# A graph attention layer's softmax taken over two batches at once, with the engines' order rewritten in pairs of batches

## The reference

```python
h = relu(layernorm(x))
q, k, v = h @ Wq + bq, h @ Wk + bk, h @ Wv + bv          # 4 heads x 32
alpha = (q[dst] * k[src]).sum(-1) / sqrt(32)             # per edge and head
ea = exp(alpha - segment_max(alpha, dst)[dst])
alpha = ea / (segment_sum(ea, dst)[dst] + 1e-16)
x = x + segment_sum(v[src] * alpha, dst) + h @ Wskip + bskip
h = relu(layernorm(x))
x = x + layer1(h, src, dst, edge_attr)
```

## Time and profile before

| | us |
|---|---|
| median of 3 runs | 1698.16 (1695.48 to 1698.21) |
| the profiled execution | 1695.94 |
| its span, first to last instruction | 1694.1 |
| PE busy | 1487.4 (88%) |
| DVE busy | 1347.4 (80%) |
| ACT busy | 1005.7 (59%) |
| POOL busy | 981.1 (58%) |

### The profile page before, as it was taken

One profiled execution on the slowest core, in us unless ns is written; L12 is line 12 of the kernel. 1 busy time (PEld: TensorE's weight loads), 2 busy tenths in 40 slices (PEclk: granted clock), 3 DMA queues, 4 the chain that ended last, 5 costly groups with the idle time before them and its releaser, 6 DMA issues.

```text
span 1694.1 us, 37116 instructions
## 1 busy us (share of the span) xinstructions
PE 1487.4 (88%) x12117; PEld 1382.1 (82%) x12118; DVE 1347.4 (80%) x3855; ACT 1005.7 (59%) x2472; POOL 981.1 (58%) x1021
## 2 busy tenths in 40 slices
PE   5877898598999999999999973899999999999996
PEld 4655676487888888888888863899999999999896
DVE  8989898288999999999999993666666666666664
ACT  5665787565665555566555521656656666565663
POOL 0110000277777777777777703777777777777772
PEclk9998999799999999999999995999999999999998
DMA  8786898746666666666666624676676766767662
GB/s 219 246 260 219 269 311 253 221 137 178 183 186 175 191 178 179 181 181 179 169 187 173 178 68 108 144 173 156 157 171 156 174 158 157 171 154 172 154 165 58
DMA packets 162139, 302.88 MB, mean 179 GB/s; under 512 B 104024, under 2 KB 107514, under 8 KB 156985
## 3 DMA queue, kind: packets, MB, share of 16 engines
q1 hardware_dynamic: 121089, 201.19, 41.3%
q0 software_dynamic: 40896, 99.90, 24.2%
HBM read 196.84 MB, written 104.12 MB: 178 GB/s over the span
## 4 chain that ended last, share of the span: by engine, by line
PE 24%; DVE 24%; POOL 18%; issue 18%; ACT 10%; DMA 4%; SPq 1%; DVEq 0%; POOLq 0%; ACTq 0%
POOL sb_kv L753 15%; PE ps_b L1572 5%; ACT sb_hn L1497 4%; ACT sb_vw L1500 4%; DVE sb_st L1115 3%; DVE sb_xo L1101 3%; PE ps_b L1669 3%; PE ps_b L1648 3%; POOL sb_kv L726 3%; DVE sb_member L1029 2%; DVE sb_alpha L1049 2%; DVE sb_kv L828 2%; DMA sb_kv<-in_x 2%; DVE sb_st L809 2%; PE ps_b L1561 2%
## 5 line engine op out<-in xcount | busy, mean ns | idle before, releaser
L726 POOL DMA_INDIRECT sb_kv<-kv_rows,sb_src_all x500 | 495.5, 991 | 375.8 <-DMA kv_rows<-sb_kv 215.3
L753 POOL DMA_INDIRECT sb_kv<-x_rows,sb_src_all x500 | 472.9, 946 | 213.9 <-issue 142.1
L1497 ACT ACTIVATE sb_hn<-sb_xn 100x128 f32<-100x128 f32 x500 | 240.4, 481 | 265.2 <-DMA sb_kv<-x_rows,sb_src_all 172.1
L1210 DVE COPY sb_hT<-ps_b 128x400 f32<-128x400 f32 x250 | 142.8, 571 | 135.0 <-PE ps_b L1757 133.8
L1425 ACT ACTIVATE sb_hn<-sb_xn,sb_nstat 100x128 f32<-100x128 f32 x500 | 231.6, 495 | 15.5 <-DMA sb_xn<-in_x 15.5
L1500 ACT ACTIVATE sb_vw<-sb_kv 128x128 f32<-128x128 f32 x500 | 239.5, 479 | 0.0
L1572 PE MATMUL ps_b<-sb_w,sb_memberT 128*125 128x256 f32 x800 | 206.4, 397 | 31.2 <-DVE sb_kv L828 18.8
L1771 PE MATMUL ps_b<-sb_w,sb_hT 128*100 128x128 f32 x1000 | 198.4, 280 | 9.7 <-DVE sb_hT L1210 9.4
L1447 ACT COPY sb_memberT<-ps_b 100x512 f32<-100x512 f32 x150 | 76.0, 507 | 207.5 <-PE ps_b L1657 207.5
L1773 PE MATMUL ps_b<-sb_weaug,sb_memberT 66*100 66x128 f32 x1000 | 193.7, 275 | 0.0
L1772 PE MATMUL ps_b<-sb_w,sb_hT 128*100 128x128 f32 x1000 | 193.3, 275 | 0.0
(11 more groups left out here) (165 smaller groups left out, 3066.4 us busy)
## 6 DMA issues: line engine op xcount, KB each, us to landing
kv_rows<-sb_kv SPq DMA_DIRECT2D x27, 1120.0 KB
x_rows<-sb_xo SPq DMA_DIRECT2D x25, 1015.6 KB
sb_xn<-x_rows SPq DMA_DIRECT2D x50, 507.8 KB
sb_xn<-in_x SPq DMA_DIRECT2D x50, 500.0 KB
out_rows<-sb_xo SPq DMA_DIRECT2D x50, 500.0 KB
sb_kv<-in_edge_attr SPq DMA_DIRECT2D x500, 32.0 KB
sb_kv<-in_x SPq DMA_DIRECT2D x28, 560.0 KB
kv_rows<-sb_xn SPq DMA_DIRECT2D x13, 1120.0 KB
```

Source lines behind the costliest of these rows:

```text
L726: pool.indirect_dma_start(out=kvs[:, k % 4, t, :], out_offset=None, in_=kv_rows, in_offset=bass.IndirectOffsetOnAxis(ap=src_all[:, n:n + 1 ...
L753: pool.indirect_dma_start(out=xs1[:, k % 4, t, :], out_offset=None, in_=x1, in_offset=bass.IndirectOffsetOnAxis(ap=src_all[:, n:n + 1], ax ...
L1497: nc.scalar.activation(hn1[:, t, :], xn1[:, k % 4, t, 0:D], ACT.Relu, scale=xn1[:, k % 4, t, D:D + 1], bias=xn1[:, k % 4, t, D + 1:XW]).th ...
```

## The change

Batches are taken in pairs (`DUOS` = 25). `alpha`, the softmax tiles and the weights have 80 rows (`TWO`) instead of 40, for batches 2p and 2p + 1; turn_alpha, the eight softmax steps, the exp, turn_weights and the load of the segment rows happen once a pair. The weighed values are written over the keys of their slot in `kvs`, so `vw` goes, and its memory holds a fourth slot of `member`. The slot in `kvs` is free for the next gather when its batch has been summed, not when it has been weighed. The offset of q is no longer a matmul in project_q: q gets a 101st row that holds bq and the turned member matrix a 101st row of ones, and gather_q contracts over 101 rows. Two DMAs write these rows once. VectorE's and TensorE's order is written anew as `second_scores(p)` and `weighed_sums(p)`; ScalarE's keeps its order but for the exp.

In this diff the old `step0` of VectorE and of TensorE, and the likewise renamed arguments of `soft_step` are left out.

```diff
+TWO = 2 * BH
+DUOS = BATCHES // 2
...
+        bqb = sb("bqb", [1, D])
...
-        qsb = q_raw[0:NODES, :].rearrange("n (s t c) -> n s t c", s=2, t=B)
-        memberT = mT_raw[0:NODES, :].rearrange("n (s t e) -> n s t e", s=2, t=B)
+        qsb = q_raw[0:NODES + 1, :].rearrange("n (s t c) -> n s t c", s=2, t=B)
+        memberT = mT_raw[0:NODES + 1, :].rearrange("n (s t e) -> n s t e", s=2, t=B)
         member = mem_raw[:].rearrange("e (s t n) -> e s t n", s=4, t=B)
-        vw = vw_raw[:].rearrange("e (t c) -> e t c", t=B)
+        member_3 = vw_raw[:, 0:B * NODES].rearrange("e (t n) -> e t n", t=B)
...
-        alpha = sb("alpha", [128, BH])
-        segk = sb("segk", [BH, 2, SEG])
-        fmax = sb("fmax", [BH, WIN])
-        smax = sb("smax", [BH, WIN])
-        dl = sb("dl", [BH, WIN])
-        er = sb("er", [BH, WIN])
-        fsum = sb("fsum", [BH, WIN])
-        tot = sb("tot", [BH, WIN])
-        tot_e = sb("tot_e", [BH, WIN])
-        rtot = sb("rtot", [BH, WIN])
-        wr = sb("wr", [BH, WIN])
+        alpha = sb("alpha", [128, TWO])
+        segk = sb("segk", [TWO, 2, SEG])
...
+        def member0(k):
+
+            return member[:, k % 4, :, :] if k % 4 < 3 else member_3
...
+            sp.dma_start(bqb[:], bq.rearrange("(o n) -> o n", o=1)).then_inc(const_load, 16)
...
-            def segments(k):
-                wait(sp, A.soft, N_SOFT * (k - 1))
-                if k == 0:
+            def segments(p):
+                wait(sp, A.soft, N_SOFT * (p - 1))
+                if p == 0:
                     sp.wait_ge(seg_out, 16)
-                rows = seg_rows[B * k:B * (k + 1), :].unsqueeze(1).to_broadcast([B, HEADS, SEG])
-                sp.dma_start(segk[:, k % 2, :], rows).then_inc(A.seg[k % 2], 16)
+                rows = seg_rows[2 * B * p:2 * B * (p + 1), :].unsqueeze(1).to_broadcast([2 * B, HEADS, SEG])
+                sp.dma_start(segk[:, p % 2, :], rows).then_inc(A.seg[p % 2], 16)
...
+            for k in range(5):
                 nodes(k)
-            for k in range(2):
-                segments(k)
-            for k in range(BATCHES + 2):
-                if k == BATCHES:
+            segments(0)
+
+            sp.wait_ge(P.hT, 3 * PB)
+            sp.dma_start(q_raw[NODES:NODES + 1, :].rearrange("o (n c) -> o n c", c=D),
+                         bqb[:].unsqueeze(1).to_broadcast([1, 2 * B, D])).then_inc(rows_set, 16)
+            sp.wait_ge(P.kv, 5 * PB)
+            sp.dma_start(mT_raw[NODES:NODES + 1, :].rearrange("o (n c) -> o n c", c=D),
+                         ones[0:1, :].unsqueeze(1).to_broadcast([1, 2 * B, D])).then_inc(rows_set, 16)
+
+            for p in range(DUOS + 1):
+                if p == DUOS - 1:
                     first_windows = window_registers(0)
-                if k >= 1 and real(k + 1):
-                    segments(k + 1)
-                if k >= 3 and k % 2 == 1:
-                    store((k - 3) // 2)
-                if real(k + 4):
-                    nodes(k + 4)
+                if p + 1 < DUOS:
+                    segments(p + 1)
+                if p >= 1:
+                    store(p - 1)
+                for k in (2 * p + 5, 2 * p + 6):
+                    if real(k):
+                        nodes(k)
...
-                wait(pool, A.vw, k - 3)
+                wait(pool, A.agg, 3 * (k - 3))
...
-                wait(dve, A.agg, 3 * (k - 2))
-                dve.tensor_tensor(member[:, k % 3, first:last, :],
+                wait(dve, A.agg, 3 * (k - 3))
+                dve.tensor_tensor(member0(k)[:, first:last, :],
...
+                wait(dve, A.aT, k // 2)
+                dve.tensor_reduce(alpha[:, BH * (k % 2):BH * (k % 2 + 1)], prod.rearrange("e t (h c) -> e (t h) c", h=HEADS), AX_X, ALU.add
...
             def weigh(k):
-                dve.wait_ge(A.wT, k + 1)
-                wait(dve, A.agg, 3 * k)
-                dve.tensor_tensor(vw.rearrange("e t (h c) -> e (t h) c", h=HEADS),
+                dve.wait_ge(A.wT, k // 2 + 1)
+                dve.wait_ge(A.prod, 3 * (k + 1))
+                weights = banks[5][:, BH * (k % 2):BH * (k % 2 + 1)]
+                dve.tensor_tensor(kvs[:, k % 4, :, 0:D].rearrange("e t (h c) -> e t h c", h=HEADS),
                                   kvs[:, k % 4, :, D:2 * D].rearrange("e t (h c) -> e t h c", h=HEADS),
-                                  banks[5][:, 0:BH].rearrange("e (t h) -> e t h", h=HEADS).unsqueeze(3)
+                                  weights.rearrange("e (t h) -> e t h", h=HEADS).unsqueeze(3)
                                   .to_broadcast([128, B, HEADS, CH]), ALU.mult).then_inc(A.vw, 1)
...
+            def second_scores(p):
+                k = 2 * p + 1
+                def stats(first, last):
+                    if p >= 1:
+                        for n in range(first, last):
+                            x1_stat_step(p - 1, n)
+                def build(part):
+                    if real(k + 2):
+                        members(k + 2, part)
+                scores(k, 0)
+                stats(0, 1)
+                scores(k, 1)
+                stats(1, 2)
+                scores(k, 2)
+                stats(2, 3)
+                head_sums(k)
+                stats(3, 4)
+                build(0)
+                stats(4, 5)
+                soft_step(p, 0)
+                stats(5, 6)
+                soft_step(p, 1)
+                stats(6, 7)
+                soft_step(p, 2)
+                stats(7, 8)
+                build(1)
+                stats(8, 9)
+                soft_step(p, 3)
+                stats(9, 10)
+                soft_step(p, 4)
+                stats(10, 11)
+                soft_step(p, 5)
+                stats(11, 12)
+                soft_step(p, 6)
+                stats(12, 13)
+                soft_step(p, 7)
+                stats(13, 14)
+            def weighed_sums(p):
+                k = 2 * p
+                nxt = real(k + 2)
+                weigh(k)
+                weigh(k + 1)
+                finish(k, 0)
+                finish(k, 1)
+                x1_stats(k, 0)
+                x1_stats(k, 1)
+                finish(k, 2)
+                x1_stats(k, 2)
                 if nxt:
+                    scores(k + 2, 0)
+                    scores(k + 2, 1)
+                finish(k + 1, 0)
                 if nxt:
+                    scores(k + 2, 2)
+                    head_sums(k + 2)
+                finish(k + 1, 1)
+                x1_stats(k + 1, 0)
+                x1_stats(k + 1, 1)
+                finish(k + 1, 2)
+                x1_stats(k + 1, 2)
+                if real(k + 4):
+                    members(k + 4, 0)
+                    members(k + 4, 1)
+            for k in range(3):
+                members(k, 0)
+                members(k, 1)
+            for g in range(3):
+                scores(0, g)
+            head_sums(0)
+            for p in range(DUOS):
+                second_scores(p)
+                weighed_sums(p)
+            for n in range(STAT_STEPS):
+                x1_stat_step(DUOS - 1, n)
...
+            def exps(p):
+                act.wait_ge(A.soft, N_SOFT * p + 3)
...
-                if real(k - 1):
-                    exps(k - 1)
...
+                if real(k) and k % 2 == 1:
+                    exps(k // 2)
...
-                nc.tensor.matmul(ps[0:NODES, 0:(last - first) * D].rearrange("n (t c) -> n t c", c=D),
-                                 ones_b[:, 0:NODES], bsplit[:, 0:D].unsqueeze(1).to_broadcast([128, last - first, D]),
-                                 start=True, stop=False)
                 for t in range(first, last):
                     ins = nc.tensor.matmul(ps[0:NODES, (t - first) * D:(t - first + 1) * D], hnT[:, k % 3, t, :],
-                                           w0[:, 0, :], start=False, stop=t == last - 1)
+                                           w0[:, 0, :], start=True, stop=True)
...
+                if a == 0:
+                    pe.wait_ge(rows_set, 32)
...
+            def turn_alpha(p):
+                pe.wait_ge(A.alpha, 2 * (p + 1))
+                wait(pe, A.vw, 2 * p)
+                nc.tensor.transpose(banks[5][0:TWO, 0:WIN], alpha[:], ident[:]).then_inc(A.aT, 1)
+
+            def turn_weights(p):
+                pe.wait_ge(A.soft, N_SOFT * (p + 1))
+                nc.tensor.transpose(banks[5][:, 0:TWO], wr[:], ident[0:TWO, 0:TWO]).then_inc(A.wT, 1)
...
-                    ins = nc.tensor.matmul(ps[0:NODES, (t - first) * D:(t - first + 1) * D], member[:, k % 3, t, :],
-                                           vw[:, t, :], start=False, stop=t == last - 1)
+                    ins = nc.tensor.matmul(ps[0:NODES, (t - first) * D:(t - first + 1) * D], member0(k)[:, t, :],
+                                           kvs[:, k % 4, t, 0:D], start=False, stop=t == last - 1)
...
+            def second_scores(p):
+                k = 2 * p + 1
+                nxt = real(k + 1)
+                gather_q(k, 2)
```

(48 more changed lines are left out.)

134 lines of the change are left out of this document (28 added, 106 removed).

## The result

| | before | changed |
|---|---|---|
| device time, median (lowest to highest) | 1696.82 us (1692.55 to 1698.21, 4 runs) | 1717.23 us (1716.07 to 1722.52, 4 runs) |
| ratio to before, with its 95% interval | 1 | 1.0122 [1.0106, 1.0137] |
| profiled execution: time, span | 1695.94, 1694.1 us | 1716.89, 1715.1 us |
| VectorE, TensorE, GpSimd busy, 600 to 700 us | 97.49, 93.92, 75.47 us | 83.62, 88.14, 72.54 us |
| one pair of batches, weighing to weighing | 26.94 us, one of 24 30.46 (mean over the layer 27.05) | 27.65 us, four of 23 29.0 to 29.2 (mean 27.91) |

The changed kernel is 1.2% slower.

A forecast was written before the change was run, and what follows sets the result against it. VectorE paces now; changed, a loop through TensorE: 23.1 work + 4.8 stalls + 0.05, 28.0 us a pair. 360.3 + 672.0 - 4.2 + 17.3 = 1045.4, 15.2 later: 1711.1 us profiled, 1713 against the median; range 1692 to 1738.

The forecast's parts named there:

- the third rival: The 80-row softmax costs twice the 40-row one, so VectorE saves nothing: loop about 29.5 us, time 1749; chance 0.03.
- (e): TensorE's turn_member(2p + 2, 2) waits for ScalarE's copy of the first four turned members: 0.64 us + 0.10.
- (d): TensorE's turn_alpha waits for the odd batch's scores and head sums: 0.31 us + 0.10.
- (a): TensorE's first aggregate waits for VectorE's weighing, no longer covered by two skips: 1.61 us, 1.71 with the weight load.
- (b): TensorE's q gather of batch 2p + 3's second four tiles waits for ScalarE's copy: 1.18 us + 0.10.
- (c): TensorE's project_q(2p + 2, 0) waits for the copy of h, without an offset matmul ahead: 0.39 us + 0.10.
- (f): TensorE's skip(2p, 2) waits for a sum: 0.14 us.
- TensorE's work, put at 23.1 us: TensorE's work for two batches: 24.6 us now, less 1.5 for the q offset and the dropped turns.
- The second rival: The clock falls in the loop behind stall (a), costing 1.7 us each; 1734 in half the pairs, 1755 in all; chance 0.18.
- an edge between 1.65 and 1.85 us: In layer 1 the clock fell after a 1.85 us stall, not after 1.65; (a) would show as about 1.6.
- the next half sentence: If the two row copies on SP's queue were late, the first q gather would wait, once.
- The tail: From the last weighing to layer 0's last layer norm step: 17.3 us, 2 of them for a falling clock.

The follow-up runs named there:

- The two runs that removed a stall each: Changed kernel with TensorE's two skips moved behind the turned weights: 1704.65 us; changed kernel with ScalarE's member copies ahead of three ReLUs: 1703.55 us.
- the run that removed both: Changed kernel with row copies ahead of later node loads, skips behind the turned weights and ScalarE's copies ahead of the ReLUs: 1672.55 us, the fastest.
- the run that put one into the kernel before: Kernel before with TensorE's two skips ahead of the turned weights instead of behind them: 1783.09 us, ratio 1.0502.

## Why the prediction was right, and where it was off

**The bound.** That VectorE's share would fall and the time rise was right, and for the reason given: the engines form a closed loop through TensorE. The two runs that removed a stall each, the run that removed both and the run that put one into the kernel before show this from four sides.

**What is taken away.** The 80-row steps have the length of the 40-row ones (the reciprocal 0.95 us, a scan 0.41), the weighing in place takes 1.49, both as taken, so the third rival is out. The offset's 1.2 us for two batches (1.1 in the run that puts it back) showed as 0.60 in the pair's length; part of the rest fell on waits, of which (e) shows 0.1 us less in that run.

**The stalls.** The view shows a wait about 0.15 us short, and one that would show as less than 0.15 not at all; so (d) has no wait of TensorE in the list above. Its weight load shows it, in each of the 20 pairs:

```profile
PEld ps_b L1708 <- DVE sb_alpha L1066: 7.2, 20, 0.5
```

From start to start, less the time of the instruction ahead, the stalls are: (a) 1.63 us where 1.61 was counted, (b) 1.06 for 1.18, (c) 0.40 for 0.39, (d) 0.31 for 0.31, (e) 0.65 for 0.64, (f) 0.17 for 0.14. In sum that is 4.22 for 4.27, so the path was right, and of the sizes only (b) is off by more than 0.03. The weight load behind a stall is open: the twelve matmuls behind (b) take 1.44 us to the next group (664.43 to 665.87), sixteen without a stall 1.79, which makes 1.34 for twelve: 0.10, as estimated. The Trainium skill (TensorE: Matmul & The Clock Gate, Part 2) has the next load pulled ahead of running matmuls; behind a stall no matmul runs, and by these 0.10 us its rule does not reach this load. The sum gave 28.0 us a pair and 27.65 was measured. The stalls explain 0.05 of the difference. Another 0.11 is in the base: 27.05 was a mean that holds the one interval of 30.46, and the pair before is 26.94 as a rule. The rest lies in TensorE's work, put at 23.1 us, and stays open.

**The clock.** The second rival came true in a small part. Stall (a) is 1.58 us in every pair, but in four of 23 the clock fell behind it, and such a pair took 29.0 to 29.2 us instead of 27.65. TensorE's timeline and the clock in one of them:

```profile
453.49 3.28 PE L1734 MATMUL ps_b<-sb_kv,sb_member 128*100 128x128 f32 x16 [1.58 <-DVE sb_kv L1107]
```

```profile
454.00:456.00 2.00, 2.00 (x12) 2.00 (x11) 1.53 (x2) 0.00 (x0) 0.96 (x2) 0.50 0.69 221
```

The sixteen products take 3.28 us, at 649.81 1.99. The price was 1.4 us where 1.7 was estimated. The sum held no falls in the loop, and with them the mean pair is 27.91 us: that this is near 28.0 is luck, two errors that cancel. The kernel of the Trainium skill (TensorE: Matmul & The Clock Gate, A second HAM failure mode), whose clock swings though its pauses are short, agrees in kind with the falls behind 1.58 us here. The prediction saw (a) as just on an edge between 1.65 and 1.85 us; the runs show no such edge. The clock fell behind stalls of 0.91 us in one run and never behind 37 of 1.58 in another, so what decides is open. Nor was it 1.00 throughout layer 0 in the kernel before: it fell at 1004.5 and 1014.8 us, near the layer's end.

**The start.** This is the step that failed: "The two row copies on SP's queue land in the 27 us in which VectorE waits for the first gathers, and cost nothing". They were issued there, but landed 18 us later; the gather waited 6.07 us, once, as the next half sentence had it, and TensorE's clock was low behind it. The first weighing came at 369.0 instead of 360.3 (whose terms, 349.67, 3.1 and 7.2, add up to 360.0), and the run with the copies issued first brought it back to 361.3. The tail was overestimated (17.3 us, measured 15.1), and the last interval was as counted (23.8 for 28.0 - 4.2). In sum: 8.7 late at the start, 2.1 less in the loop, 2.2 less behind it, and 1.4 more in layer 1, which was taken as untouched: 5.8 more, and the profiled execution took 1716.9 for the 1711.1 of the sum.

**GpSimd.** It waits for sums 2.0 us a pair (1 to 2 foreseen), and nobody waits for it. Its reserve was overestimated, as the run with the later slot shows.

## What to carry to other kernels

When engines lie within 10% of each other, as here, taking work from the busiest one is only half of an edit: follow two rounds by hand for what covers each handover, and keep independent work (here the two skips) between a producer's request and the wait for its answer. The same saving lost 1.2% or won 1.5% by the order of a dozen instructions on two engines and of two copies on SyncE's queue. A small transfer that something will wait for is issued ahead of large ones on its queue, however much idle time seems to be there. And a usual interval is compared with a usual one: a mean took in one odd interval of 30.46 us.

## What was unexpected of the hardware

- Of 23 stalls of the same 1.58 us, with the same instructions around them, four were followed by 1.2 GHz, 167.3 us apart, which is every sixth pair; in the run with the rows first there were four as well, in other pairs, and with the gap filled and the stall at 0.92 us none. But in the run with the skips behind the turned weights the clock fell twice behind a stall of 0.91 us, which stood 2.2 us behind one of 0.52, and in the kernel before with its skips ahead it fell behind none of 37 stalls of 1.58 us. The length of the stall alone does not decide.
- Two copies of 10 KB behind 2.5 MB of loads on the same queue landed some 18 us after their issue; issued behind one load of the five, their packets were done within 5 us.
- With products that nobody reads, 0.66 us of them in a gap of 1.6, the loop was 5.6 us shorter, by the four falls that did not come.
- The pace of gathers is 1.31 us each, of which 0.30 is the time between two of them on GpSimd: the share of 76% that the busy column gives to GpSimd in the fastest kernel is an engine at its limit.
